# Pair-product ring of five PSUM banks instead of six, with the eighth bank given to attention and residuals

## The chip, the core and the metric

The kernel runs on one core of a Trainium2 chip. The metric is the device time of one execution in microseconds (us). Engines: PE (TensorE), with its weight load shown as PEld; DVE (VectorE); ACT (ScalarE); POOL (GpSimd); SP (SyncE), which issues DMAs. They run side by side and are ordered by semaphores. PSUM has eight banks of 128 partitions x 512 f32. PE writes its results there, DVE and ACT read them.

## What is computed

64 graphs of 128 nodes with 128 features. Cut to what matters:

```python
# layer 0, per graph: x, adj are 128 x 128
h   = relu(hi[:, None, :] + hj[None, :, :] + b1)     # 128 x 128 pairs x 128
y   = layernorm(h @ W2 + b2) * gamma + beta          # over the last axis
x1  = layernorm(x + einsum('ij,ijh->ih', adj, y))
# layer 1
e     = exp(si[:, None] + sj[None, :] + a_b) * adj
x_out = layernorm(x1 + (e / e.sum(1, keepdims=True)) @ x1)
```

## The kernel before, in words

All is f32 but a scratch tile of squares. The program is unrolled over 66 slots, t = 0 to 65 (`run_slots`, L156). In slot t three graphs are at work: the *pairs* of graph t (slots 0 to 63), the *gather* of graph t-1 (its layer norm statistics and the weighted sums over pairs) and the *tail* of graph t-2 (residual, layer norms, attention). *prep* prepares graph t+1. Slots 2 to 63 have pairs, gather and tail.

A slot has 16 units u of 8 rows i, and a unit has two quarts k of 4 rows. A quart goes through the engines like this:

- POOL (L278) adds hi and hj for a unit into `h`. ACT (L294) applies the relu in place, two units ahead of use.
- PE (L650, issued in the helper line L567) multiplies the quart by `w_pair` into one PSUM bank of the ring `y_ps`: 4 products, 32 matmul instructions in the trace, over four column tiles. Ahead of a unit it waits for `h_ready`, and ahead of quart k for `q_done >= t*QUARTS + k - YRING + 1` (L645), which says that DVE is through with the bank's earlier contents.
- ACT (L367, in the trace L289) copies the quart from the bank to `y` in SBUF.
- DVE (L553) multiplies bank and copy and sums the products into `q`: four instructions per quart, each followed by a read of the accumulator. The last one counts up `q_done`. DVE's code goes by (u, e), e = 0 to 3: e = 0, 1 are the halves of quart 2u, and e = 2, 3 those of quart 2u+1. A step at (u, e) stands ahead of that half's squares.

Between the quarts, at fixed places, stand the steps of gather and tail, in program order on each engine:

- DVE: variance `v` at (0,0), L449; the diagonal blocks of the sums into `o_sb` and `o_all` at (0,0) to (0,3), L460 to L468; `adj_sum` at (1,0), L455; `x1p` (gamma, mean and bias part) at (2,0), (2,1), (2,2), L476, L479, L483; x1p plus residual and its statistics at (4,0) to (4,2), L489 to L497; x1 and the two scores at (6,0) to (6,2), with the transposes for the next graph; `project`, the copy of the projections, at (9,0); attention's row sum, inverse and residual at (11,0) to (11,3); statistics at (12,0), (12,1); output at (14,0).
- ACT: `ln_v` and `rstd` at u = 1, `beta_part` at 2, the first root at 6, exponentials and `x1s` at 8, the second root at 14.
- POOL: weights `wz` at u = 5, `x_beta` at 6.
- PE: projections of the next graph at u = 9 (L631), attention at u = 11 (L638), and behind the pairs of units 4, 6, 7, 9, 10, 12, 13 and 15 one chunk of the weighted sums (L618), eight matmul instructions of 512 columns. The first chunk waits for `wz` and for L483 of the tail.

PSUM: six banks are the ring `y_ps` (the last of them also serves the setup), one is `agg_ps` (weighted sums), and one is `work_ps`. That one holds `v`, then attention `att` over the same columns, `z_e`, `z_r`, `x1p` (later `ab_ps`, the projections, over it) and `x2p`. Several engines use `work_ps`, so extra waits keep their steps apart: L475 (ln_v has read v before x1p is written), L630 and L635 on PE.

Of the kernel before, what the change touches and what calls it, by code (L numbers as in the profile page):

```python
# [33 lines left out]
def gnn_pair_kernel(nc, x, adj, W1, b1, W2, b2, gamma, beta, Ww, Wb, aw, ab, out):  # L34
# [4 lines left out]
    B, S, H = x.shape  # L39
    K = W2.shape[0]  # L40
# [6 lines left out]
    HRING = 4  # L47
    YRING = 6
    GROUPS, GROUP = 4, 32
# [13 lines left out]
    with ctx:  # L63
# [55 lines left out]
        agg_ps = ps("agg_ps", [S, 512])  # L119
        work_ps = ps("work_ps", [S, 512])  # L120
        setup_ps = y_ps[YRING - 1]
        v = work_ps[:, 0:K]
        att = work_ps[:, 0:K + 1]
        z_e, z_r = work_ps[:, K + 1:K + 2], work_ps[:, K + 2:K + 3]
        x1p, x2p = work_ps[:, 2 * K:3 * K], work_ps[:, 3 * K:4 * K]
        ab_ps = work_ps[:, 2 * K:4 * K].rearrange("k (m s) -> k m s", m=2)
# [160 lines left out]
        def _(act):  # L287
# [21 lines left out]
            def slot(t, half, p, pairs, prep, gather, tail, early, first_bank):  # L309
                for u in range(UNITS):  # L310
# [30 lines left out]
                    if tail and u == 8:  # L341
# [8 lines left out]
                        nc.scalar.activation(x1s[:], x1e[:], ACT.Identity, scale=e_ij[:, 1:2]).then_inc(x1s_ready, 1)  # L350
                    if tail and u == 14:

                        act.wait_ge(mv2_ready, t - 1)
                        nc.scalar.activation(ln2[:], mv2[:, 1:2], ACT.Ln, bias=epsc[:, 0:1]).then_inc(ln2_ready, 1)
                        act.wait_ge(ln2_ready, t - 1)
                        nc.scalar.activation(rs2[:], ln2[:], ACT.Exp, scale=-0.5).then_inc(rs2_ready, 1)  # L356
# [17 lines left out]
        def _(dve):  # L374
# [66 lines left out]
            def slot(t, half, p, pairs, prep, gather, tail, early, first_bank):  # L441

                for u, e in ((u, e) for u in range(UNITS) for e in range(2 * QPU)):
# [17 lines left out]
                    if tail and u == 0 and 1 <= e < CHUNK:  # L461
# [5 lines left out]
                        else:  # L467
                            nc.vector.scalar_tensor_tensor(out=o_all, in0=agg_ps[:, e * K:(e + 1) * K], scalar=part[:, e:e + 1],  # L468
                                                           in1=o_sb[:], op0=ALU.mult, op1=ALU.add,
                                                           accum_out=o_sum[:, 0:1]).then_inc(o_stored, 1)  # L470
                    if tail and (u, e) == (2, 0):
                        dve.wait_ge(o_stored, t - 1)
                        if gather:

                            dve.wait_ge(ln_v_ready, t)  # L475
                        nc.vector.tensor_tensor(x1p, o_all, gamma_rows[:], ALU.mult).then_inc(scaled_ready, 1)  # L476
                    if tail and (u, e) == (2, 1):
                        dve.wait_ge(scaled_ready, t - 1)
                        nc.vector.scalar_tensor_tensor(out=x1p, in0=mean_rows[:], scalar=o_sum[:, 0:1], in1=x1p,  # L479
                                                       op0=ALU.mult, op1=ALU.add).then_inc(mean_added, 1)  # L480
                    if tail and (u, e) == (2, 2):
                        dve.wait_ge(mean_added, t - 1)
                        nc.vector.scalar_tensor_tensor(out=x1p, in0=bias_rows[:], scalar=o_all[:, LAST:S], in1=x1p,  # L483
                                                       op0=ALU.mult, op1=ALU.add).then_inc(bias_added, 1)
# [27 lines left out]
                    if prep and (u, e) == (9, 0):  # L512
# [3 lines left out]
                        project(t + 1, 1 - p)  # L516
                    if tail and (u, e) == (11, 0):
                        dve.wait_ge(att_done, t - 1)
                        dve.wait_ge(e_ready, t - 1)
                        nc.vector.tensor_scalar(z_e, att[:, K:K + 1], e_ij[:, 0:1], None, ALU.mult).then_inc(z_e_ready, 1)  # L520
                    if tail and (u, e) == (11, 1):
                        dve.wait_ge(z_e_ready, t - 1)
                        nc.vector.reciprocal(z_r, z_e).then_inc(z_r_ready, 1)
                    if tail and (u, e) == (11, 2):
                        dve.wait_ge(z_r_ready, t - 1)
                        nc.vector.tensor_scalar(rz[:], z_r, e_ij[:, 0:1], None, ALU.mult).then_inc(rz_ready, 1)
                    if tail and (u, e) == (11, 3):
                        dve.wait_ge(rz_ready, t - 1)
                        dve.wait_ge(x1_ready, t - 1)
                        nc.vector.scalar_tensor_tensor(out=x2p, in0=att[:, 0:K], scalar=rz[:, 0:1], in1=x1e[:, 0:K],  # L530
                                                       op0=ALU.mult, op1=ALU.add).then_inc(x2p_ready, 1)
                    if tail and (u, e) == (12, 0):
                        dve.wait_ge(x2p_ready, t - 1)
                        nc.vector.bn_stats(st2[:], x2p).then_inc(st2_ready, 1)
                    if tail and (u, e) == (12, 1):
                        dve.wait_ge(st2_ready, t - 1)

                        dve.sem_inc(s_passed, 1)
                        nc.vector.bn_aggr(mv2[:], st2[:]).then_inc(mv2_ready, 1)
                    if tail and (u, e) == (14, 0):  # L540
                        dve.wait_ge(rs2_ready, t - 1)
# [21 lines left out]
        def _(pe):  # L563
# [58 lines left out]
            def slot(t, half, p, pairs, prep, gather, tail, early, first_bank):  # L622
                for u in range(UNITS):
                    if prep and u == 9:
                        if gather:

                            pe.wait_ge(ln_v_ready, t)
                        if tail:

                            pe.wait_ge(sj_ready, t - 1)  # L630
                        prep_products(t + 1, True)  # L631
                    if tail and u == 11:
                        if prep:

                            pe.wait_ge(ab_sb_s, t + 2)  # L635
                        pe.wait_ge(x1s_ready, t - 1)
# [49 lines left out]
```

## Time and profile before

| | |
|---|---|
| median of 3 runs | 2303.24 us (2301.99 to 2304.12) |
| the profiled execution | 2303.22 us |
| its span | 2301.4 us |
| PE, ACT, DVE, POOL busy | 99%, 94%, 93%, 88% |
| mean granted TensorE clock | 0.998 |

The span runs from the first to the last instruction of the trace; the rest of the time lies around it. Busy shares are averages over the span. The end of a matmul is modelled. Times in the rows are microseconds from the span's start.

### The profile page before, as it was taken

How to read it: one execution, taken by the hardware profiler on the slowest of the kernel's cores; microseconds unless marked ns; L12 is line 12 of the kernel's file. 1: busy time of each engine (PE TensorE's matmuls, PEld its weight loads, DVE VectorE, ACT ScalarE, POOL GpSimd, SP SyncE). 2: the span in 40 equal slices, each digit the busy share in tenths (PEclk: the TensorE clock that was granted, in tenths of full speed). 3: DMA queues.
4: the chain of work that ended last, by engine and by line, in shares of the span. 5: the costliest groups of instructions: out<-in, count | busy, mean ns of one | idle time of the engine just before them, and what ended most of it. 6: DMA issues, size and time to landing. Idle time of an engine off the chain costs nothing.

```text
span 2301.4 us, 168989 instructions
## 1 busy us (share of the span) xinstructions
PE 2280.2 (99%) x71248; PEld 2075.6 (90%) x71248; DVE 2145.2 (93%) x18262; ACT 2160.9 (94%) x3650; POOL 2016.9 (88%) x1227
## 2 busy tenths in 40 slices
PE   8999999999999999999999999999999999999997
PEld 8888888888888999999999999999999999999995
DVE  7999999999999999999999999999999999999998
ACT  8999999999999999999999999999999999999996
POOL 9898898888988988888888898898888988888884
PEclk9999999999999999999999999999999999999999
DMA  1000000000000000000000000000000000000000
GB/s 21 12 13 16 11 16 16 10 16 12 15 16 10 16 16 11 16 12 15 16 11 16 13 13 16 11 16 16 10 16 13 14 16 10 16 17 10 16 10 10
DMA packets 103862, 32.15 MB, mean 14 GB/s; under 512 B 77888, under 2 KB 103104, under 8 KB 103104
## 3 DMA queue, kind: packets, MB, share of 16 engines
q1 hardware_dynamic: 102240, 21.12, 4.4%
q8 instruction: 561, 9.19, 1.7%
q14 instruction: 197, 1.61, 0.2%
q10 hardware_dynamic: 864, 0.23, 0.0%
HBM read 17.11 MB, written 4.19 MB: 9 GB/s over the span
## 4 chain that ended last, share of the span: by engine, by line
PE 97%; ACT 2%; DVE 1%; POOL 0%; issue 0%; DMA 0%; SPq 0%; DVEq 0%; ACTq 0%
PE y_ps L567 76%; PE agg_ps L618 19%; PE work_ps L567 2%; ACT h L294 1%; ACT y L289 1%; POOL h L278 0%; DVE squares L553 0%; DMA b1c<-in_L_gnn_b_dram 0%; DVE o_sb L465 0%; DVE x_out L545 0%; POOL wz L269 0%; SPq L172 0%; DVE work_ps L483 0%; DVE work_ps L530 0%; DVE work_ps L479 0%
## 5 line engine op out<-in xcount | busy, mean ns | idle before, releaser
L278 POOL TENSOR_TENSOR h<-abT 128x1024 f32<-128x1024 f32 x1024 | 1944.0, 1919 | 239.3 <-PE y_ps L567 231.9
L567 PEld LDWEIGHTS y_ps<-w_pair,h 128*32 128x32 f32 x65536 | 1920.4, 110 | 173.6 <-issue 126.5
L567 PE MATMUL y_ps<-w_pair,h 128*32 128x128 f32 x65536 | 1966.0, 273 | 1.3 <-issue 0.6
L553 DVE CUSTOM_DVE_ANT_0 squares<-y_ps,y 128x128 bf16<-128x128 f32 x8192 | 1839.0, 284 | 110.4 <-ACT y L289 103.4
L289 ACT ACTIVATE y<-y_ps 128x508 f32<-128x508 f32 x2048 | 1137.5, 596 | 104.6 <-PE y_ps L567 97.6
L294 ACT ACTIVATE h<-h 128x1024 f32<-128x1024 f32 x1024 | 1089.3, 1064 | 2.4 <-POOL h L278 2.4
L553 DVE DVE_READ_ACCUMULATOR2_ANT q<- 128x1 f32 x8192 | 678.5, 83 | 0.0
L618 PE MATMUL agg_ps<-y,wz 128*32 128x512 f32 x4096 | 593.4, 592 | 3.2 <-DVE work_ps L483 3.1
L618 PEld LDWEIGHTS agg_ps<-y,wz 128*32 128x32 f32 x4096 | 180.4, 110 | 9.1 <-issue 9.1
L567 PEld LDWEIGHTS work_ps<-x1s,adjS 128*32 128x32 f32 x512 | 28.4, 110 | 31.5 <-issue 18.9
L252 POOL TENSOR_TENSOR wz<-adjT,rstd 128x128 f32<-128x128 f32 x64 | 34.8, 543 | 25.0 <-ACT rstd L325 25.0
L545 DVE TENSOR_SCALAR x_out<-work_ps,mv,rs 128x128 f32<-128x128 f32 x64 | 26.2, 410 | 27.5 <-ACT rs L356 27.5
L465 DVE SCALAR_TENSOR_TENSOR o_sb<-agg_ps,part,o_sb 128x128 f32<-128x128 f32 x128 | 44.3, 346 | 0.1
L567 PE MATMUL work_ps<-x1s,adjS 128*32 128x129 f32 x512 | 33.8, 275 | 6.4 <-ACT x1s L350 6.4
L264 POOL TENSOR_TENSOR x_beta<-beta_part,x_res 128x128 f32<-128x128 f32 x64 | 29.7, 464 | 10.4 <-ACT beta_part L334 10.4
L567 PE MATMUL work_ps<-xT,w1a 128*32 128x128 f32 x512 | 33.6, 275 | 4.4 <-DMA b1c<-in_L_gnn_b_dram 4.4
L567 PE MATMUL work_ps<-xT,w1b 128*32 128x128 f32 x512 | 33.6, 275 | 0.0
L334 ACT ACTIVATE beta_part<-beta_rows,adj_sum 128x128 f32<-128x128 f32 x64 | 25.7, 401 | 3.0 <-DVE adj_sum L455 3.0
L350 ACT ACTIVATE x1s<-x1e,e_ij 128x129 f32<-128x129 f32 x64 | 25.9, 405 | 2.1
L500 DVE TENSOR_SCALAR x1e<-work_ps,mv,rs 128x128 f32<-128x128 f32 x64 | 26.1, 407 | 1.2 <-ACT rs L340 1.2
L567 PEld LDWEIGHTS work_ps<-xT,w1a 128*32 128x32 f32 x512 | 22.5, 110 | 4.4 <-issue 4.4
L506 DVE CUSTOM_DVE_ANT_0 s_terms<-work_ps,v2row,score_c 128x128 f32<-128x128 f32 x64 | 26.1, 407 | 0.0
(87 smaller groups left out, 591.3 us busy)
## 6 DMA issues: line engine op xcount, KB each, us to landing
adj_in<-in_adj_dram SPq DMA_DIRECT2D x256, 16.0 KB, 1.9
x_res<-in_x_dram SPq DMA_DIRECT2D x64, 64.0 KB, 2.1
adj_res<-in_adj_dram SPq DMA_DIRECT2D x64, 64.0 KB, 2.7
out_dram<-x_out SPq DMA_DIRECT2D x64, 64.0 KB, 1.9
x_in<-in_x_dram SPq DMA_DIRECT2D x254, 16.0 KB, 1.9
w1a<-in_L_gnn_W_dram SPq DMA_DIRECT2D x1, 64.0 KB, 1.9
w1b<-in_L_gnn_W_dram ACTq DMA_DIRECT2D x1, 64.0 KB, 2.2
w<-in_L_gnn_W_dram ACTq DMA_DIRECT2D x1, 64.0 KB, 2.3
```

What stands on the lines that cost most here:

```text
L252: nc.gpsimd.tensor_tensor(columns, adjT[:, 1 - p, :].rearrange("j (g c s) -> j g c s", g=GROUPS, s=CHUNK), rstd[:].rearrange("j (c s g) -> ...
L264: nc.gpsimd.tensor_tensor(x_beta[:], beta_part[:], x_res[:, p, :], ALU.add).then_inc(x_beta_ready, 1)
L278: nc.gpsimd.tensor_tensor(h[:, u % HRING].rearrange("k (r g) s -> k r g s", g=GROUPS), abT[:, p, 1, :].unsqueeze(1).unsqueeze(1).broadcast ...
L289: return nc.scalar.activation(dst, src, ACT.Copy)
L294: nc.scalar.activation(h[:, u % HRING], h[:, u % HRING], ACT.Relu).then_inc(h_ready, 1)
L465: nc.vector.scalar_tensor_tensor(out=o_sb[:], in0=agg_ps[:, e * K:(e + 1) * K], scalar=part[:, e:e + 1], in1=o_sb[:], op0=ALU.mult, op1=AL ...
L500: nc.vector.tensor_scalar(x1e[:, 0:K], x1p, mv1[:, 0:1], rs1[:, 0:1], ALU.subtract, ALU.mult).then_inc(x1_ready, 1)
L506: nc.vector.tensor_tensor_reduce(out=s_terms[:, 0, :], in0=x1p, in1=v2row[:], scale=rs1[:, 0:1], scalar=score_c[:, 0:1], op0=ALU.mult, op1 ...
L545: nc.vector.tensor_scalar(x_out[:], x2p, mv2[:, 0:1], rs2[:, 0:1], ALU.subtract, ALU.mult).then_inc(out_ready, 1)
L553: last = nc.vector.tensor_tensor_reduce(out=squares[:, (first_bank + k) % YRING, n, :], in0=y_ps[(first_bank + k) % YRING][:, n, :], in1=y ...
L567: last = nc.tensor.matmul(dst[cols], lhsT[:, cols], rhs, start=start, stop=stop, tile_position=(0, g * GROUP))
L618: last = nc.tensor.matmul(agg_ps[g * GROUP:(g + 1) * GROUP, :], wz[:, g, chunk, :], y_chunk[:, :, g, :], start=(chunk == 0), stop=(chunk = ...
```

## The change

The ring has five banks, so PE waits for `q_done` of quart k-5. The freed bank is `att_ps` and takes `att`, `z_e`, `z_r`, `x1p` and `x2p`; `v` and `ab_ps` stay in `work_ps`. The three x1p steps on DVE stand at (1,1), (1,2), (1,3) in place of (2,0), (2,1), (2,2). Attention on PE is at u = 10 in place of 11, and the steps that follow from it stand one unit earlier: on DVE at 10, 11 and 13, on ACT the second root at 13. Three waits are gone: for `ln_v_ready` ahead of x1p, for `sj_ready` ahead of the projections, for `ab_sb_s` ahead of attention. `setup_ps`, the ring's last bank, is number 4 in place of 5.

```diff
--- before.py
+++ after.py
@@ -45,7 +45,7 @@
     QUARTS = S // QUART
     QPU = UNIT // QUART
     HRING = 4
-    YRING = 6
+    YRING = 5
     GROUPS, GROUP = 4, 32
     LAST = S - 1
 
@@ -117,12 +117,12 @@
 
         y_ps = [ps(f"y_ps{n}", [S, QUART, K]) for n in range(YRING)]
         agg_ps = ps("agg_ps", [S, 512])
-        work_ps = ps("work_ps", [S, 512])
+        work_ps, att_ps = ps("work_ps", [S, 512]), ps("att_ps", [S, 512])
         setup_ps = y_ps[YRING - 1]
         v = work_ps[:, 0:K]
-        att = work_ps[:, 0:K + 1]
-        z_e, z_r = work_ps[:, K + 1:K + 2], work_ps[:, K + 2:K + 3]
-        x1p, x2p = work_ps[:, 2 * K:3 * K], work_ps[:, 3 * K:4 * K]
+        att = att_ps[:, 0:K + 1]
+        z_e, z_r = att_ps[:, K + 1:K + 2], att_ps[:, K + 2:K + 3]
+        x1p, x2p = att_ps[:, 2 * K:3 * K], att_ps[:, 3 * K:4 * K]
         ab_ps = work_ps[:, 2 * K:4 * K].rearrange("k (m s) -> k m s", m=2)
         o_all = agg_ps[:, 0:K]
         b2c_ps, bnorm_ps = agg_ps[:, 3 * K:3 * K + 1], setup_ps[:, 3, 4:5]
@@ -348,7 +348,7 @@
                         act.wait_ge(e_ready, t - 1)
                         act.wait_ge(x1_ready, t - 1)
                         nc.scalar.activation(x1s[:], x1e[:], ACT.Identity, scale=e_ij[:, 1:2]).then_inc(x1s_ready, 1)
-                    if tail and u == 14:
+                    if tail and u == 13:
 
                         act.wait_ge(mv2_ready, t - 1)
                         nc.scalar.activation(ln2[:], mv2[:, 1:2], ACT.Ln, bias=epsc[:, 0:1]).then_inc(ln2_ready, 1)
@@ -468,17 +468,14 @@
                             nc.vector.scalar_tensor_tensor(out=o_all, in0=agg_ps[:, e * K:(e + 1) * K], scalar=part[:, e:e + 1],
                                                            in1=o_sb[:], op0=ALU.mult, op1=ALU.add,
                                                            accum_out=o_sum[:, 0:1]).then_inc(o_stored, 1)
-                    if tail and (u, e) == (2, 0):
+                    if tail and (u, e) == (1, 1):
                         dve.wait_ge(o_stored, t - 1)
-                        if gather:
-
-                            dve.wait_ge(ln_v_ready, t)
                         nc.vector.tensor_tensor(x1p, o_all, gamma_rows[:], ALU.mult).then_inc(scaled_ready, 1)
-                    if tail and (u, e) == (2, 1):
+                    if tail and (u, e) == (1, 2):
                         dve.wait_ge(scaled_ready, t - 1)
                         nc.vector.scalar_tensor_tensor(out=x1p, in0=mean_rows[:], scalar=o_sum[:, 0:1], in1=x1p,
                                                        op0=ALU.mult, op1=ALU.add).then_inc(mean_added, 1)
-                    if tail and (u, e) == (2, 2):
+                    if tail and (u, e) == (1, 3):
                         dve.wait_ge(mean_added, t - 1)
                         nc.vector.scalar_tensor_tensor(out=x1p, in0=bias_rows[:], scalar=o_all[:, LAST:S], in1=x1p,
                                                        op0=ALU.mult, op1=ALU.add).then_inc(bias_added, 1)
@@ -514,30 +511,30 @@
 
                             dve.wait_ge(u_ready, t * UNITS)
                         project(t + 1, 1 - p)
-                    if tail and (u, e) == (11, 0):
+                    if tail and (u, e) == (10, 0):
                         dve.wait_ge(att_done, t - 1)
                         dve.wait_ge(e_ready, t - 1)
                         nc.vector.tensor_scalar(z_e, att[:, K:K + 1], e_ij[:, 0:1], None, ALU.mult).then_inc(z_e_ready, 1)
-                    if tail and (u, e) == (11, 1):
+                    if tail and (u, e) == (10, 1):
                         dve.wait_ge(z_e_ready, t - 1)
                         nc.vector.reciprocal(z_r, z_e).then_inc(z_r_ready, 1)
-                    if tail and (u, e) == (11, 2):
+                    if tail and (u, e) == (10, 2):
                         dve.wait_ge(z_r_ready, t - 1)
                         nc.vector.tensor_scalar(rz[:], z_r, e_ij[:, 0:1], None, ALU.mult).then_inc(rz_ready, 1)
-                    if tail and (u, e) == (11, 3):
+                    if tail and (u, e) == (10, 3):
                         dve.wait_ge(rz_ready, t - 1)
                         dve.wait_ge(x1_ready, t - 1)
                         nc.vector.scalar_tensor_tensor(out=x2p, in0=att[:, 0:K], scalar=rz[:, 0:1], in1=x1e[:, 0:K],
                                                        op0=ALU.mult, op1=ALU.add).then_inc(x2p_ready, 1)
-                    if tail and (u, e) == (12, 0):
+                    if tail and (u, e) == (11, 0):
                         dve.wait_ge(x2p_ready, t - 1)
                         nc.vector.bn_stats(st2[:], x2p).then_inc(st2_ready, 1)
-                    if tail and (u, e) == (12, 1):
+                    if tail and (u, e) == (11, 1):
                         dve.wait_ge(st2_ready, t - 1)
 
                         dve.sem_inc(s_passed, 1)
                         nc.vector.bn_aggr(mv2[:], st2[:]).then_inc(mv2_ready, 1)
-                    if tail and (u, e) == (14, 0):
+                    if tail and (u, e) == (13, 0):
                         dve.wait_ge(rs2_ready, t - 1)
                         if early >= 3:
 
@@ -625,14 +622,8 @@
                         if gather:
 
                             pe.wait_ge(ln_v_ready, t)
-                        if tail:
-
-                            pe.wait_ge(sj_ready, t - 1)
                         prep_products(t + 1, True)
-                    if tail and u == 11:
-                        if prep:
-
-                            pe.wait_ge(ab_sb_s, t + 2)
+                    if tail and u == 10:
                         pe.wait_ge(x1s_ready, t - 1)
                         pe.wait_ge(adjS_ready, t - 1)
                         mm(att, adjS[:, p, :], x1s[:]).then_inc(att_done, 1)
```

## Rows read from the trace of the kernel before

**Rows 1.** The page: busy us (share of the span) and instructions of each engine

```profile
PE 2280.2 (99%) x71248; PEld 2075.6 (90%) x71248; DVE 2145.2 (93%) x18262; ACT 2160.9 (94%) x3650; POOL 2016.9 (88%) x1227
```

**Rows 2.** Chain that ended last, longest pieces: start us, us, what

```profile
77.39 8.73 PE y_ps L567 x320
112.86 8.73 PE y_ps L567 x320
...
2101.56 8.88 PE y_ps L567 x312
```

**Rows 3.** All waits in one slot, 1000 to 1036: who for whom, us, times, longest

```profile
POOL h L278 <- PE y_ps L567: 3.7, 6, 0.9
DVE squares L553 <- ACT y L289: 1.8, 4, 0.8
ACT y L289 <- PE y_ps L567: 1.5, 6, 0.4
DVE x_out L545 <- ACT rs L356: 0.4, 1, 0.4
POOL wz L252 <- ACT rstd L325: 0.3, 1, 0.3
```

**Rows 4.** Windows, L567 alone: busy us and instructions (x), granted clock

```profile
1000.17:1007.18 7.01, 7.01 (x256) 7.01 (x256) 1.00 0.19 40
```

**Rows 5.** Windows, two whole slots: busy us of each engine, granted clock

```profile
1000.17:1035.64 35.47, 35.47 (x1117) 33.03 (x1112) 33.48 (x286) 33.71 (x58) 31.50 (x20) 1.00 0.06 13
1035.64:1071.91 36.27, 35.86 (x1117) 32.98 (x1113) 33.46 (x286) 34.02 (x58) 31.48 (x20) 1.00 0.06 14
```

**Rows 6.** Timeline, weight load ahead of the first sums of the slot: start us, us

```profile
1008.79 0.15 PEld L618 LDWEIGHTS agg_ps<-y,wz 128*32 128x32 f32 x3
```

**Rows 7.** Timeline, the matmuls of the same instructions

```profile
1008.90 0.63 PE L618 MATMUL agg_ps<-y,wz 128*32 128x512 f32 x3
```

**Rows 8.** Timeline, DVE in units 1, 2 and 4: start us, us, line, operation

```profile
1005.85 0.08 DVE L553 DVE_READ_ACCUMULATOR2_ANT q<- 128x1 f32 x1
...
1006.69 0.08 DVE L553 DVE_READ_ACCUMULATOR2_ANT q<- 128x1 f32 x1
1006.69 0.29 DVE L476 TENSOR_TENSOR work_ps<-agg_ps,gamma_rows 128x128 f32<-128x128 f32 x1
1007.16 0.29 DVE L553 CUSTOM_DVE_ANT_0 squares<-y_ps,y 128x128 bf16<-128x128 f32 x1 [0.17 <-ACT y L289]
...
1007.59 0.35 DVE L479 SCALAR_TENSOR_TENSOR work_ps<-mean_rows,o_sum,work_ps 128x128 f32<-128x128 f32 x1
1007.85 0.28 DVE L553 CUSTOM_DVE_ANT_0 squares<-y_ps,y 128x128 bf16<-128x128 f32 x1
...
1008.27 0.08 DVE L553 DVE_READ_ACCUMULATOR2_ANT q<- 128x1 f32 x1
...
1012.30 0.09 DVE L553 DVE_READ_ACCUMULATOR2_ANT q<- 128x1 f32 x1
```

**Rows 9.** Timeline, set-up: DVE releases a weight load

```profile
6.23 0.28 DVE L417 COPY w2T<-y_ps 128x128 f32<-128x128 f32 x1
...
6.57 0.20 PEld L567 LDWEIGHTS agg_ps<-basis,w2T 128*32 128x32 f32 x8 [0.99 <-DVE w2T L417]
```

**Rows 10.** Timeline, drain: DVE releases the sums

```profile
2281.73 0.36 DVE L483 SCALAR_TENSOR_TENSOR work_ps<-bias_rows,agg_ps,work_ps 128x128 f32<-128x128 f32 x1
...
2282.21 0.19 PEld L618 LDWEIGHTS agg_ps<-y,wz 128*32 128x32 f32 x8 [3.96 <-issue]
2282.24 1.06 PE L618 MATMUL agg_ps<-y,wz 128*32 128x512 f32 x8 [3.08 <-DVE work_ps L483]
```

**Rows 11.** Timeline, PE at the second chunk of sums

```profile
1013.25 0.63 PE L618 MATMUL agg_ps<-y,wz 128*32 128x512 f32 x3
```

**Rows 12.** Timeline, weight loads in slot 1

```profile
48.92 1.69 PEld L567 LDWEIGHTS y_ps<-w_pair,h 128*32 128x32 f32 x64 [0.74 <-ACT h L294]
```

**Rows 13.** Timeline, DVE in slot 1, the end of quart 4

```profile
50.24 0.08 DVE L553 DVE_READ_ACCUMULATOR2_ANT q<- 128x1 f32 x1
```

## The prediction, made before the changed kernel was run

> **What bounds the kernel now.** Start with the busy table [rows 1]: PE is busy 99% of the span, ACT 94%, DVE 93%, POOL 88%. Busy PE time is modelled, so it proves nothing alone. The chain of work that ended last [rows 2] goes by PE nearly throughout, and its pieces repeat: 320 matmuls of the pair product in one unbroken piece of 8.73 us, and the next such piece starts 35.47 us later (112.86 - 77.39). Then read the waits of one slot [rows 3]: POOL, ACT and DVE wait for PE (3.7 and 1.5 us) or for each other, and no line has PE or its weight load waiting. The windows [rows 5] say the same: 35.47 us of a slot, 35.47 us of PE. So in a steady slot PE streams without a stall, at a granted clock of 1.00, and any stall that the change puts into PE's stream is paid in full, once per slot. For the same reason nothing can be won by taking away a wait of PE that is already met.
>
> I call a bank's worth of rows a quart (four rows i, 32 matmul instructions). A slot has 32 quarts, two to a unit. From [rows 4], 256 matmuls, which is quarts 0 to 7, fill 7.01 us from the slot's start at 1000.17. So quart 8 starts at 1007.18 and quart 9 at 1008.05, 0.87 us each. PE loads weights 0.11 us ahead of the matmul (1008.79 against 1008.90, [rows 6, 7]), and the wait sits on the first weight load. So the loads that the waits hold stand at about 1007.07 (quart 8) and 1007.94 (quart 9).
>
> **The ring, six to five.** L645 lets PE write quart k when DVE has squared quart k-6. With five banks it is k-5, which is one quart, 0.87 us, less lead. Where is DVE furthest behind? In units 0 to 2 of a slot it has the tail's work between its squares. DVE's timeline [rows 8] gives the ends. L476 stands ahead of quart 4's first square, so quart 3 ended at 1006.69 + 0.08 = 1006.77. Four squares earlier, at a pitch of 0.21, quart 2 ended at 1005.85 + 0.08 = 1005.93. Quart 4 starts at 1007.16, takes four pitches and L479, and ends at 1008.27 + 0.08 = 1008.35. With six banks quart 9 needs quart 3 (1006.77 against 1007.94: 1.17 us in hand). With five it needs quart 4: 1008.35 is 0.41 us after the load wants to go. Quart 8 needs quart 3: 0.30 us in hand. So with the ring alone one wait per slot appears, at quart 9.
>
> How long from DVE's end to PE's load? The trace of before has no wait of PE on squares. The nearest rows [rows 9, 10]: w2T ends at 6.51 and the load starts at 6.57 (0.06); L483 ends at 2282.09 and the load of the sums starts at 2282.21 (0.12). I take 0.09. There the matmul follows the released load by 0.03 us, not 0.11, so about 0.1 us of a late load is absorbed by the lead. The ring alone: 0.41 + 0.09 - 0.10 = 0.40 us per slot.
>
> **The x1p chain moved from unit 2 to unit 1.** L476, L479 and L483 now stand ahead of half-quarts (1,1), (1,2) and (1,3), so one lies inside quart 2 and two ahead of the halves of quart 3. What one inserted step costs DVE is the distance to the next square [rows 8]: 0.26 us for L479 (1007.59 to 1007.85), and the same for L483, which has its form. L476 lasts 0.29 us, as a square does, so I give it the square's pitch, 0.21. Quart 2 ends 0.21 later (1006.14; quart 7's load wants 1006.20, so with 0.06 to 0.12 of release up to 0.06 late, and I fold that into what follows). Quart 3 ends 0.73 later: 1007.50. Nothing absorbs this: four squares in 0.84 us are back to back. The 0.17 us that DVE idles ahead of quart 4 [rows 8] lies behind it.
>
> So quart 8's load, which needs quart 3, goes at 1007.50 + 0.09 = 1007.59 in place of 1007.07, and its matmul at about 1007.61 in place of 1007.18: 0.43 us late. Quart 4: its first square goes at 1006.69 + 0.73 = 1007.42 (the copy is done by 1007.16), its last read ends after four pitches of 0.21 and 0.08 at 1008.34, the same as before, since the three steps are now ahead of it. Quart 9's load may go at 1008.43. PE, already late, wants it at 1007.61 + 0.87 - 0.11 = 1008.37, so 0.06 more, most of it within the lead; I add 0.03. **0.46 us per slot.** Quart 5 ends 0.2 us earlier than before, and the next tight place is quart 13, which needs quart 8: done at 1012.30 + 0.09 = 1012.39 [rows 8], and its load stands at 1013.25 - 0.87 - 0.11 = 1012.27 [rows 11]. That is 0.12 short today and is covered once PE is 0.46 late. So the stalls don't add up, the first one pays for the others. ACT lags there: DVE gets the copy of quart 4 at 1007.16, and PE had started the last matmul of that quart by 1000.17 + 5 x 0.87 = 1004.5. So ACT doesn't feel PE's delay. POOL waits for PE in six places of a slot [rows 3]; I take it that none of them leads back to PE within the slot. By the end of a slot everyone waits for PE again and the slot starts as before.
>
> **The split of the banks.** PE loses its wait for sj_ready ahead of the projections and for ab_sb_s ahead of attention; L476 loses the wait for ln_v_ready. In a steady slot no engine stands on any of them [rows 3]: worth 0. Attention one unit earlier: the same eight matmuls. z_e to bn_aggr in units 10 and 11, ln2 and rs2 in 13: the same instructions, at places where DVE and ACT themselves wait for PE [rows 3]. They are the cover, and 0.2 to 0.3 us per step would show only if it were gone. No DMA is moved. In the drain (slots 64 and 65) attention goes ahead of a chunk of sums and DVE's chain ends earlier, but DVE then waits for PE's last sums: 0.1 us gained at most.
>
> **The first slots.** The setup bank is now bank 4, so PE waits for s_ready one quart earlier, but L435 had long ended. In slots 0 and 1 ACT sets the pace: quart 8 of slot 1 starts at 48.92 released by ACT's h [rows 12]. Quart 9's load wants about 49.7, and quart 4 ends at 50.24 + 0.08 = 50.32 [rows 13]. So PE leaves this stretch about 0.6 us later, once (0 to 1).
>
> The trace shows 0.11 us from load to matmul [rows 6, 7]. The Trainium skill ("TensorE: Matmul & The Clock Gate", Part 2, step by step) says that PE takes weight loads ahead of running matmuls out of a queue of 64. If a load held by a wait could be passed that far, the whole 0.46 us would hide, and the time would be (c) below; the 0.11 us speaks for only a quarter of it.
>
> **The sum.** Steady slots with both pairs and a tail are t = 2 to 63, 62 of them. 62 x 0.46 = 28.5; start +0.6; drain -0.1; in all +29.0. The profiled execution took 2303.22 us, 2301.4 of them span, within 0.02 of the median 2303.24, so it stands for the median. 2303.2 + 29.0 = 2332.2, 1.3% slower.
>
> **The rivals.**
> (a) The forecast, one stall per slot at quart 8 or 9. Bounds per slot: from 0.34 (release 0.06, ring alone, lead of 0.13) to 0.62 (release 0.12, nothing absorbed): 21 to 38 us, and up to 1 at the start. 2324 to 2343. The ring alone, 0.40, would give 2328.6, so both parts of the change lead into this range. Chance 0.78.
> (b) The stalls add up: PE, late at quart 8, delays POOL and ACT's relu of later units so that quart 13 and later ones are late as well. For it: ACT has little room (94%). Against it: ACT is over 2 us behind PE at quart 4 [rows 8]. A second stall of the same size gives 62 x 0.9 = 56: about 2360. Chance 0.08.
> (c) The stall is hidden, same time: DVE's lag at quart 3 is regained, or the load's lead swallows it. That would need less than 0.07 us per slot in place of 0.46. Time 2303 to 2307. Against it: 0.41 us short at quart 9 is read off two rows. Chance 0.11.
> (d) Faster: PE's waits at units 9 and 11 for DVE (sj_ready) and for abT (ab_sb_s) cost something in the slots that are longer than 35.47 us, such as that from 1035.64 to 1071.91 (36.27 us, 35.86 of PE) [rows 5]. It would have to give over 5 us, and the ring to cost nothing. But from the piece at 77.39 to that at 2101.56 there are 57 slots in 2024.17 us [rows 2], and 57 x 35.47 = 2021.8: all the longer ones together hold 2.4 us. With all of it back: 2301. Chance 0.03.
> The rule to have all 8 PSUM banks in use (the Trainium skill, "Perfetto Trace Analysis", Matmul Optimizations) sees no difference, since both kernels use eight; by it the result would be (c). The trace speaks of the six and five that rotate.
>
> **How the numbers follow.** The likeliest is (a) at 2332. Its own range is 2324 to 2343; to hold 8 in 10 I widen it a little for slots whose stall is smaller or larger than in the one that I read: 2320 to 2346. A measurement of this kernel can tell about 0.2% (4.6 us). Slower is (a) and (b) and a sliver of (c): 0.87; same is most of (c) and of (d): 0.11; faster 0.02.
>
> **What would show it.** In the trace after: the slot's pitch at 35.9 to 36.0 us; in the list of waits PE or its weight load waiting for DVE squares L553, about 62 times, 0.3 to 0.5 us each; the unbroken piece of 320 matmuls cut at 256; quart 3 of a slot ending 0.7 us later. Wrong: a pitch of 35.47 with these waits absent (c); the stall at two places (b); or a wait of PE on something else.

## The result, and the profile after

| | before | after |
|---|---|---|
| median | 2303.68 us (4 runs) | 2325.53 us (4 runs) |
| ratio, 95% interval | | 1.0097 (1.0085 to 1.011) |
| profiled execution, its span | 2303.22, 2301.4 us | 2324.8, 2322.9 us |
| busy PE / DVE / ACT / POOL | 99 / 93 / 94 / 88% | 99 / 93 / 93 / 87% |

The changed kernel is 21.9 us slower, 1.0%. I had forecast 2332 (2320 to 2346). The busy table, to be held against [rows 1], and the chain's shares by engine, after:

```profile
PE 2292.5 (99%) x71248; PEld 2003.7 (86%) x71248; DVE 2162.6 (93%) x18262; ACT 2166.8 (93%) x3650; POOL 2016.7 (87%) x1227
...
PE 73%; DVE 20%; ACT 6%; issue 1%; POOL 0%; DMA 0%; SPq 0%; DVEq 0%; ACTq 0%
```

PE is still "99% busy", as before. The chain tells the two apart: before, PE held 97% of it, and now PE holds 73% and DVE 20%. Here is one slot of the chain of work that ended last in the changed kernel (start, length, what; "..." marks pieces left out), to be held against [rows 2]:

```profile
1045.38 0.29 DVE squares L550
...
1050.89 0.21 DVE att_ps L473
...
1051.51 0.27 DVE att_ps L476
...
1052.18 0.27 DVE att_ps L480
...
1053.02 1.95 PE y_ps L564 x64
1054.97 0.86 PE agg_ps L615 x8
...
1079.16 0.59 ACT y L289
...
1080.70 0.49 ACT y L289
```

The slot begins with DVE. From 1045.38 to about 1052.9 the chain is its squares with the tail's steps between them, up to L480 (the lines L473, L476 and L480 of this kernel are L476, L479 and L483 of the kernel before). At 1053.02, at quart 8, it goes over to PE and stays there for 26 us, until ACT's copies at 1079.16 and 1080.70 lead to DVE's squares of the next slot. In [rows 2] PE's piece ran unbroken through quarts 0 to 9.

The same place on PE (matmuls) and on the weight load, in the timeline of the changed kernel:

```profile
1045.66 7.20 PE L564 MATMUL y_ps<-w_pair,h 128*32 128x128 f32 x256
1053.02 1.95 PE L564 MATMUL y_ps<-w_pair,h 128*32 128x128 f32 x64 [0.16 <-DVE q L550]
```

```profile
1045.66 6.93 PEld L564 LDWEIGHTS y_ps<-w_pair,h 128*32 128x32 f32 x252 [0.27 <-issue]
1052.99 1.72 PEld L564 LDWEIGHTS y_ps<-w_pair,h 128*32 128x32 f32 x64 [0.40 <-issue]
```

```profile
1081.50 7.20 PE L564 MATMUL y_ps<-w_pair,h 128*32 128x128 f32 x256
1088.85 1.41 PE L564 MATMUL y_ps<-w_pair,h 128*32 128x128 f32 x44 [0.15 <-DVE q L550]
```

The piece of 320 matmuls is cut at 256, as the forecast had said. Quart 8 starts 1053.02 - 1045.66 = 7.36 us into the slot (7.35 in the next slot), where it started after 7.01 us before [rows 4]. The slot's pitch is 1081.50 - 1045.66 = 35.84 us, before 35.47: 0.37 us more. In slots 2 to 20 of the kernel before, and in ring5_alone, quart 8 starts at 6.99 (medians), and 7.36 - 6.99 is 0.37, so all of the slot's loss lies at this one place. And DVE's end of quart 3, in its timeline:

```profile
1050.80 0.30 DVE L473 TENSOR_TENSOR att_ps<-agg_ps,gamma_rows 128x128 f32<-128x128 f32 x1
1051.00 0.28 DVE L550 CUSTOM_DVE_ANT_0 squares<-y_ps,y 128x128 bf16<-128x128 f32 x1
...
1051.42 0.35 DVE L476 SCALAR_TENSOR_TENSOR att_ps<-mean_rows,o_sum,att_ps 128x128 f32<-128x128 f32 x1
1051.68 0.29 DVE L550 CUSTOM_DVE_ANT_0 squares<-y_ps,y 128x128 bf16<-128x128 f32 x1
...
1052.10 0.36 DVE L480 SCALAR_TENSOR_TENSOR att_ps<-bias_rows,agg_ps,att_ps 128x128 f32<-128x128 f32 x1
1052.36 0.29 DVE L550 CUSTOM_DVE_ANT_0 squares<-y_ps,y 128x128 bf16<-128x128 f32 x1
...
1052.79 0.09 DVE L550 DVE_READ_ACCUMULATOR2_ANT q<- 128x1 f32 x1
```

Quart 3's last read ends at 1052.79 + 0.09 = 1052.88, PE's held load starts at 1052.99. [rows 8] shows the first two of the three steps before, in unit 2.

A reader who looks for the stall in the list of waits of the whole kernel finds little of it under its own name:

```profile
PEld y_ps L564 <- issue: 235.2, 845, 0.7
...
PE y_ps L564 <- DVE q L550: 9.0, 56, 0.4
```

62 slots times 0.37 us is 23 us, and the list has 9.0 us (56 times) for the matmul waiting for DVE. The weight load's idle of 0.40 us at 1052.99 goes to "issue", whose sum grew from 126.5 us, on the page before, to 235.2. The matmuls' own row hides part of the gap, too: their ends are modelled, and the piece of 256 is shown 7.20 us long where the pace of [rows 4] gives 7.01. The chain and the place where a regular pattern is cut were the views that found it.

The start: slot 2 began at 77.21 us with slot 0 at 9.84 before, and now

```profile
9.88 18.18 PE L564 MATMUL y_ps<-w_pair,h 128*32 128x128 f32 x574
...
77.85 7.17 PE L564 MATMUL y_ps<-w_pair,h 128*32 128x128 f32 x256
```

that is 67.97 us in place of 67.37, or 0.6 us more, once. It doesn't come about at one place. Quart 4 of slot 0 starts 4.46 us into the slot, before 5.54, because PE went over from 1.69 to 0.87 us a quart earlier in this execution, for a reason that no row shows. From quart 9 on the ring holds PE already in slot 0, as here:

```profile
19.21 1.75 PEld L564 LDWEIGHTS y_ps<-w_pair,h 128*32 128x32 f32 x64 [0.40 <-DVE q L550]
```

Slot 1 starts 0.87 us later than before, and within slot 1 0.28 us of that is regained.

### The profile page after: what moved, and what is told of

Its sections match the earlier page's. It is cut to its first block, busy times and chain, and to the rows that moved or that the text cites. A ratio compares the mean times of both kernels' runs of the same rounds, so it can differ in the third digit from the quotient of the medians.

```text
span 2322.9 us, 168866 instructions
## 1 busy us (share of the span) xinstructions
PE 2292.5 (99%) x71248; PEld 2003.7 (86%) x71248; DVE 2162.6 (93%) x18262; ACT 2166.8 (93%) x3650; POOL 2016.7 (87%) x1227
## 4 chain that ended last, share of the span: by engine, by line
PE 73%; DVE 20%; ACT 6%; issue 1%; POOL 0%; DMA 0%; SPq 0%; DVEq 0%; ACTq 0%
PE y_ps L564 54%; PE agg_ps L615 17%; DVE squares L550 12%; ACT y L289 3%; ACT h L294 3%; DVE o_sb L465 1%; PE work_ps L564 1%; DVE q L550 1%; DVE work_ps L449 1%; DVE agg_ps L468 1%; DVE att_ps L480 1%; DVE att_ps L476 1%; DVE o_sb L460 1%; PE att_ps L564 1%; DVE att_ps L473 1%
## 5 line engine op out<-in xcount | busy, mean ns | idle before, releaser
L564 PEld LDWEIGHTS y_ps<-w_pair,h 128*32 128x32 f32 x65536 | 1845.5, 110 | 259.4 <-issue 235.2
L564 PE MATMUL y_ps<-w_pair,h 128*32 128x128 f32 x65536 | 1930.7, 273 | 10.5 <-DVE q L550 9.0
L615 PE MATMUL agg_ps<-y,wz 128*32 128x512 f32 x4096 | 550.7, 592 | 3.2 <-DVE att_ps L480 3.2
L615 PEld LDWEIGHTS agg_ps<-y,wz 128*32 128x32 f32 x4096 | 142.3, 110 | 8.2 <-issue 8.2
L564 PEld LDWEIGHTS att_ps<-x1s,adjS 128*32 128x32 f32 x512 | 21.2, 110 | 39.9 <-issue 31.6
L564 PE MATMUL att_ps<-x1s,adjS 128*32 128x129 f32 x512 | 28.7, 275 | 6.2 <-ACT x1s L350 6.2
L542 DVE TENSOR_SCALAR x_out<-att_ps,mv,rs 128x128 f32<-128x128 f32 x64 | 26.3, 412 | 5.6 <-ACT rs L356 1.2
L497 DVE TENSOR_SCALAR x1e<-att_ps,mv,rs 128x128 f32<-128x128 f32 x64 | 26.2, 410 | 3.3 <-ACT rs L340 1.2
L503 DVE CUSTOM_DVE_ANT_0 s_terms<-att_ps,v2row,score_c 128x128 f32<-128x128 f32 x64 | 26.1, 407 | 0.0
L320 ACT ACTIVATE ln_v<-work_ps,epsc 128x128 f32<-128x128 f32 x64 | 23.4, 366 | 2.4 <-DVE work_ps L449 2.4
```

The source lines that it names most:

```text
L497: nc.vector.tensor_scalar(x1e[:, 0:K], x1p, mv1[:, 0:1], rs1[:, 0:1], ALU.subtract, ALU.mult).then_inc(x1_ready, 1)
L503: nc.vector.tensor_tensor_reduce(out=s_terms[:, 0, :], in0=x1p, in1=v2row[:], scale=rs1[:, 0:1], scalar=score_c[:, 0:1], op0=ALU.mult, op1 ...
L542: nc.vector.tensor_scalar(x_out[:], x2p, mv2[:, 0:1], rs2[:, 0:1], ALU.subtract, ALU.mult).then_inc(out_ready, 1)
L564: last = nc.tensor.matmul(dst[cols], lhsT[:, cols], rhs, start=start, stop=stop, tile_position=(0, g * GROUP))
L615: last = nc.tensor.matmul(agg_ps[g * GROUP:(g + 1) * GROUP, :], wz[:, g, chunk, :], y_chunk[:, :, g, :], start=(chunk == 0), stop=(chunk = ...
```

## The experiments

Each is compared with the kernel before on the same chip. "Pitch" is the distance from one slot's first pair matmul to the next one's, which stays the same over most slots of a run.

| kernel | ring | pitch, us | median, us | ratio to before |
|---|---|---|---|---|
| before | 6 | 35.47 | 2303.7 | |
| after | 5 | 35.84 | 2325.5 | 1.0097 (1.0085 to 1.011) |
| ring5_alone | 5 | 35.73 | 2320.5 | 1.0073 (1.0057 to 1.009) |
| x1p_early_ring6 | 6 | 35.47 | 2303.9 | 0.9998 (0.9988 to 1.0007) |
| x1p_back_ring5 | 5 | 35.73 | 2320.5 | 1.007 (1.0055 to 1.0085) |
| relieved | 5 | 35.47 | 2304.8 | 1.0006 (0.9996 to 1.0015) |
| ring4 | 4 | 36.68 | 2379.4 | 1.0335 (1.0318 to 1.0352) |
| one_more_step | 5 | 36.03 | 2339.1 | 1.016 (1.0144 to 1.0175) |
| one_more_step_ring6 | 6 | 35.47 | 2303.8 | 1.0003 (0.9994 to 1.0013) |
| attention_early_ring6 | 6 | 35.79 | 2321.6 | 1.0084 (1.0069 to 1.0099) |
| x1p_spread | 5 | 35.64 | 2319.2 | 1.0066 (1.0051 to 1.0081) |
| beta_late | 5 | 35.47 | 2306.0 | 1.001 (1.000 to 1.0019) |
| x1p_placed | 5 | 35.48 | 2307.7 | 1.0014 (1.0005 to 1.0023) |

Theory R says that the cost is PE's wait for DVE's squares of quart k-5, and nothing else. Rival C says that it is the x1p chain's earlier place.

### The ring alone

```diff
--- before
-    YRING = 6
+    YRING = 5
```

> The kernel before with five ring banks and nothing else; the eighth bank lies unused, all waits and places are the old ones. Theory R (the ring's wait on DVE's squares is the whole cost): one stall per slot at quart 9, which now needs quart 4. Quart 4 ends 0.41 us after quart 9's weight load wants to go, release 0.12 as in the changed kernel, some 0.1 absorbed by the lead: pitch 35.47 + 0.43, in all about +25 us, 2328. Rival C (the x1p chain, put earlier on DVE, is what costs): it is at its old place here, so the time stays within 5 us of before.

Measured: 2320.5, +16.9 us. The ring by itself costs, so rival C falls as the whole cause. The size is below the 25 us that I expected. The weight loads at quart 9, and DVE:

```profile
1016.10 0.81 PEld L567 LDWEIGHTS y_ps<-w_pair,h 128*32 128x32 f32 x32 [0.32 <-DVE q L553]
```

```profile
1014.39 0.08 DVE L553 DVE_READ_ACCUMULATOR2_ANT q<- 128x1 f32 x1
...
1015.96 0.08 DVE L553 DVE_READ_ACCUMULATOR2_ANT q<- 128x1 f32 x1
```

```profile
1008.00 9.18 PE L567 MATMUL y_ps<-w_pair,h 128*32 128x128 f32 x320
```

```profile
1043.73 9.18 PE L567 MATMUL y_ps<-w_pair,h 128*32 128x128 f32 x320
```

Quart 4 ends at 1015.96 + 0.08 = 1016.04, and the load follows at 1016.10, 0.06 us later. The slot starts at 1008.00, so quart 4 ends 8.04 us into it, where I had read 1008.35 - 1000.17 = 8.18 in the slot of [rows 8]. Pitch 1043.73 - 1008.00 = 35.73: 0.26 us per slot in place of 0.40.

### The x1p steps early, with six banks

```diff
--- before
-                    if tail and (u, e) == (2, 0):
+                    if tail and (u, e) == (1, 1):
...
-                    if tail and (u, e) == (2, 1):
+                    if tail and (u, e) == (1, 2):
...
-                    if tail and (u, e) == (2, 2):
+                    if tail and (u, e) == (1, 3):
```

> The kernel before, six ring banks, with only the three x1p steps moved to unit 1 (their wait for ln_v_ready stays). Theory R: quart 9 needs quart 3, which ends 0.7 us later but still 0.4 us before the load wants to go: pitch 35.47, time within 3 us of before. Rival C: the moved chain costs by itself, pitch about 35.8, +20 us.

Measured: 2303.9, no difference. With six banks the early chain is free. Its wait for ln_v_ready stood in this kernel, so that wait, which the split removes, is met as well.

### The x1p steps late, with five banks

```diff
--- after
-                    if tail and (u, e) == (1, 1):
+                    if tail and (u, e) == (2, 0):
...
-                    if tail and (u, e) == (1, 2):
+                    if tail and (u, e) == (2, 1):
...
-                    if tail and (u, e) == (1, 3):
+                    if tail and (u, e) == (2, 2):
```

> The changed kernel with the x1p steps back in unit 2. Theory R: the stall moves from quart 8 to quart 9 and keeps its size within 0.05 us, since quart 4 ends at the same time either way: pitch 35.80 to 35.88, 2324 to 2328. Rival C: the stall at quart 8 came of the moved chain, so it goes: near 2304.

Measured: 2320.5. The stall moved to quart 9, but it didn't keep its size: the pitch is 35.73, below the 35.80 to 35.88 that I expected, and equal to that of the ring alone. So of the 0.37 us, the ring costs 0.26 with the x1p steps where they were, and their earlier place adds 0.10, about 5 us in all. It adds them only because the ring has five banks. ring5_alone and x1p_back_ring5 differ in the bank split, the waits and attention's place, and have the same pitch and time: these parts are worth nothing here.

### One more step on DVE, with five banks and with six

```diff
--- after, and x1p_early_ring6
                         dve.wait_ge(o_stored, t - 1)
+                        nc.vector.tensor_tensor(spare[:], o_all, gamma_rows[:], ALU.mult)
                         nc.vector.tensor_tensor(x1p, o_all, gamma_rows[:], ALU.mult).then_inc(scaled_ready, 1)
```

`spare` is a new tile in SBUF that nobody reads. With six banks the wait for ln_v_ready stands between the first two lines.

> The changed kernel with one more DVE step of L476's kind at (1,1), written to a spare tile in SBUF that nobody reads. Theory R: quart 3 ends 0.21 us later and PE stands at it, so the pitch grows by that much, 35.83 to 36.04, and the time by 62 x 0.21 = 13 us to about 2338. Rival (each stall has a price of its own, such as restarting PE's stream, whatever its length): the time stays within 2 us of the changed kernel, 2325.

> Six ring banks, one bank for attention and variance, x1p steps in unit 1 with their old wait, and the same additional DVE step at (1,1). Theory R: quart 9 needs quart 3, which now ends at 7.51 us of the slot, with release 7.63, and the load wants to go at 7.79: nothing, pitch 35.47, 2304. Rival (DVE's load counts, whatever the ring): +13 us as with five banks.

Measured: 2339.1 and 2303.8. Slots in the timelines of PE:

```profile
1051.92 7.20 PE L566 MATMUL y_ps<-w_pair,h 128*32 128x128 f32 x256
...
1087.95 7.20 PE L566 MATMUL y_ps<-w_pair,h 128*32 128x128 f32 x256
```

```profile
999.59 9.00 PE L569 MATMUL y_ps<-w_pair,h 128*32 128x128 f32 x317
...
1035.06 9.00 PE L569 MATMUL y_ps<-w_pair,h 128*32 128x128 f32 x317
```

Pitch 36.03 with five banks and 35.47 with six. The additional 0.2 us of DVE comes out one to one in the slot with five banks (36.03 - 35.84 = 0.19) and not at all with six. That rules out a fixed price for each stall and also DVE's load as such.

### Four banks

```diff
--- after
-    YRING = 5
+    YRING = 4
```

> The changed kernel with four ring banks. Theory R, from the trace of the changed kernel: quart 7 then needs quart 3, which ends 7.27 us into the slot, 0.12 of release makes 7.39, and quart 7's load wants to go at 6.03: 1.36 late, 0.1 absorbed. Quart 8 then needs quart 4 (8.12 + 0.12) and PE, already late, wants it at 8.24: no more. So again one stall pays for all: pitch 35.47 + 1.25 = 36.7, 2380 to 2390 in all. Rival (stalls add up, as DVE and ACT fall behind with PE): well over 2400. Rival (cost in proportion to banks taken away): pitch 35.47 + 2 x 0.36 = 36.2, about 2349.

Measured: 2379.4, just under the range that I gave, pitch 36.68, or 1.21 us over that of six banks: close to the 1.25 that came from two ends in the trace of the changed kernel, and far from both rivals. The weight loads in one slot (start, length):

```profile
1037.56 0.81 PEld L564 LDWEIGHTS y_ps<-w_pair,h 128*32 128x32 f32 x32 [0.35 <-DVE q L550]
1038.86 0.84 PEld L564 LDWEIGHTS y_ps<-w_pair,h 128*32 128x32 f32 x32 [0.48 <-issue]
1040.16 2.62 PEld L564 LDWEIGHTS y_ps<-w_pair,h 128*32 128x32 f32 x96 [0.46 <-DVE q L550]
```

and the matmuls:

```profile
1032.91 5.74 PE L564 MATMUL y_ps<-w_pair,h 128*32 128x128 f32 x192
...
1040.17 2.89 PE L564 MATMUL y_ps<-w_pair,h 128*32 128x128 f32 x96 [0.19 <-DVE q L550]
```

Quarts 5, 6 and 7 each start late. Without a stall quart 7 starts 6.11 us into the slot and quart 8 at 6.99 (medians in ring5_alone). Here quart 7 starts at 1040.17 - 1032.91 = 7.26, 1.15 late, and quart 8 at 8.20 (median of all slots), 1.21 late: the 0.06 that quart 8 adds, where I had expected none, doesn't show as a gap of its own. What counts is the largest of "DVE's end of quart k-4, less the time at which PE would want quart k"; here quarts 7 and 8 are nearly level and quart 8 is the last. The stalls of one slot don't add up beyond it.

### Relief ahead of quart 4

On POOL `x_beta`, on ACT `beta_part`, and on DVE the x1p steps:

```diff
--- after
-    POOL_WEIGHTS_UNIT, POOL_RESIDUAL_UNIT = 5, 6
+    POOL_WEIGHTS_UNIT, POOL_RESIDUAL_UNIT = 5, 7
...
-                    if tail and u == 2:
+                    if tail and u == 3:
...
-                    if tail and (u, e) == (1, 1):
+                    if tail and (u, e) == (2, 0):
...
-                    if tail and (u, e) == (1, 2):
+                    if tail and (u, e) == (2, 2):
...
-                    if tail and (u, e) == (1, 3):
+                    if tail and (u, e) == (2, 3):
```

> The changed kernel with DVE and ACT relieved ahead of quart 4: x1p steps at (2,0), (2,2), (2,3), beta_part on ACT at unit 3 in place of 2, x_beta on POOL at unit 7 in place of 6. Theory R: quart 3 then ends 0.27 us before quart 8's load wants to go and quart 4, no longer held by ACT's beta_part, ends about 0.2 us before quart 9's: the stall goes, pitch 35.47 to 35.55, 2303 to 2309, with five banks. If the time stays near 2325, the number of banks costs in another way than by these two quarts.

Measured: 2304.8, 1.0006 (0.9996 to 1.0015), pitch 35.47. Five banks cost nothing per slot once the first five quarts are ready in time. The next two kernels take this one apart.

`x1p_spread` has only the x1p steps of the diff above.

> The changed kernel with the x1p steps at (2,0), (2,2), (2,3) and nothing else moved, beta_part back at unit 2. Theory R: quart 4 is held by ACT's copy until 6.85 us into the slot, but L479 no longer lies inside it: it ends at 7.78 in place of 8.04, release makes 7.84, and quart 9's load wants to go at 7.75. 0.09 late is within what PE absorbs: pitch 35.47 to 35.52, 2303 to 2307. If it is near 2312, ACT's copy was half of the stall and beta_part had to move too.

Measured: 2319.2. This missed, and in a third place. The chain of waits of this kernel, in a slot:

```profile
1114.44 8.73 PE y_ps L564 x320
1123.18 1.03 PE agg_ps L615 x8
...
1127.70 0.86 PE agg_ps L615 x8
```

The 320 matmuls of quarts 0 to 9 are whole again, so the ring's stall is gone. But the first chunk of sums takes 1.03 us where every other takes 0.86: 0.17 us per slot. PE waits there for L480, the last x1p step, which my expectation had left out. The timelines of DVE and of the weight load:

```profile
1014.98 0.36 DVE L480 SCALAR_TENSOR_TENSOR att_ps<-bias_rows,agg_ps,att_ps 128x128 f32<-128x128 f32 x1
```

```profile
1015.45 0.11 PEld L615 LDWEIGHTS agg_ps<-y,wz 128*32 128x32 f32 x1
```

L480 ends at 1015.34, 8.76 us into the slot that starts at 1006.58, and the load of the sums starts at 1015.45. In the kernel relieved, where the x1p steps stand at the same places, L480 ends 0.2 us earlier in the slot (median), since ACT's copy of quart 4 comes 0.2 us earlier there.

`beta_late` has only the POOL and ACT lines of the diff, with the x1p steps at (2,0), (2,1), (2,2).

> The changed kernel with the x1p steps back at (2,0), (2,1), (2,2), and beta_part on ACT at unit 3, x_beta on POOL at unit 7. Theory R: ACT's copy of quart 4 is 0.3 us earlier, quart 4 starts at 6.62 in place of 6.85 and ends, with L479 inside, at 7.80 in place of 8.04; release 7.86 against 7.75: 0.11 late, about what PE absorbs: pitch 35.47 to 35.55, 2303 to 2309. If ACT is not what holds quart 4, the stall stays: pitch 35.73, 2320.

Measured: 2306.0, pitch 35.47. With `beta_part` behind quarts 4 and 5, ACT's copy of quart 4 starts 5.95 us into the slot in place of 6.23 (medians; x1p_back_ring5 has the same x1p places), and the stall that x1p_back_ring5 had is gone. So ACT, not DVE alone, held quart 4. `x_beta` was moved with `beta_part`, which it reads; no run moves one alone.

### The x1p steps at the places that both waits allow

```diff
--- after
-                    if tail and (u, e) == (1, 1):
+                    if tail and (u, e) == (1, 3):
...
-                    if tail and (u, e) == (1, 2):
+                    if tail and (u, e) == (2, 0):
...
-                    if tail and (u, e) == (1, 3):
+                    if tail and (u, e) == (2, 2):
```

> The changed kernel with the x1p steps at (1,3), (2,0), (2,2); all else as changed. It asks whether the 0.17 us per slot that the spread placement kept is PE's first chunk of sums waiting for the last x1p step, L480, which then ended 8.76 us into the slot, while the chunk's load wants to go at 8.62. Here L480 stands one half-quart earlier and ends near 8.1. Quart 3 ends at 6.68, quart 8's load wants 6.88; quart 4 ends near 7.80, release 7.86, quart 9's load wants 7.75 and absorbs that. If the chunk's wait was the rest: pitch 35.47 to 35.50, 2303 to 2307, with five banks and the x1p steps alone moved. If not, the pitch stays at 35.64, near 2319.

Measured: 2307.7, pitch 35.48. Both waits are gone but for 0.01 us per slot. Moving three steps by two or three half-quarts gives back 18 of the 22 us. The ratio, 1.0014 (1.0005 to 1.0023), leaves some 3 us, of which the pitch explains 0.6. In the profiled execution the rest lies mostly in the drain: from slot 63 to the end it took 60.7 us, the profiled kernel before 57.7. Here are the sums of slot 64, first in x1p_placed, then in the kernel before:

```profile
2283.96 6.59 PE L615 MATMUL agg_ps<-y,wz 128*32 128x512 f32 x32 [3.19 <-DVE att_ps L480]
...
2290.59 3.62 PE L615 MATMUL agg_ps<-y,wz 128*32 128x512 f32 x32
```

```profile
2282.24 4.50 PE L618 MATMUL agg_ps<-y,wz 128*32 128x512 f32 x40 [3.08 <-DVE work_ps L483]
```

and the window from 2284 to 2288 in the same order (length, then busy us and instructions of PE, PEld, DVE, ACT and POOL, then the granted clock):

```profile
2284.00:2288.00 4.00, 4.00 (x20) 1.05 (x24) 1.71 (x8) 1.11 (x4) 0.00 (x0) 0.50 0.02 4
```

```profile
2284.00:2288.00 4.00, 4.00 (x48) 1.59 (x44) 1.64 (x9) 0.61 (x2) 0.00 (x0) 1.00 0.00 0
```

PE had waited 3.19 us for L480, and 3.08 us in the kernel before. In x1p_placed the granted clock then stood at 0.50, the lower of its two levels (1.2 GHz), and 32 sums took 6.59 us where the next 32 took 3.62. In the kernel before it was 1.00 in this window. The profiled x1p_spread (6.56 us for those 32 sums), relieved, beta_late and x1p_back_ring5 (5.34 each) show it too, and that is part of what their times have above their pitches. So does x1p_early_ring6 (6.20 us for 40 sums, against 4.50), which has six banks, so this remainder isn't the ring's. Why the clock fell after one such wait and not after the other stays open, and so does how often it does in the executions without a profile.

### Attention one unit earlier in one shared bank

```diff
--- before
-                    if tail and u == 11:
+                    if tail and u == 10:
                         if prep:
                             pe.wait_ge(ab_sb_s, t + 2)
```

The steps at 11, 12 and 14 on DVE and at 14 on ACT are one unit earlier in the same way.

> The kernel before, six ring banks and one bank for variance, projections and attention, with attention and what follows from it one unit earlier (places 10, 11 and 13) and its wait for ab_sb_s kept. It asks what the split of the banks buys. PE wants attention's first load 20.9 us into the slot, where quart 20's load stands; DVE ends the copy of the projections at 21.8: PE's load 0.9 us late, some 0.4 of it absorbed by the load's lead behind the 512-column sums. Pitch 35.47 + 0.5 to 0.6, 2330 to 2345. If the wait is met earlier than I read, 2304.

Measured: 2321.6, pitch 35.79, 0.32 per slot in place of 0.5 to 0.6, so the time is below the range that I gave. The mechanism is as expected:

```profile
1030.03 0.16 PEld L567 LDWEIGHTS work_ps<-x1s,adjS 128*32 128x32 f32 x8 [1.02 <-DVE abT L396]
```

```profile
1029.63 0.34 DVE L396 TENSOR_SCALAR abT<-work_ps,b1c 128x128 f32<-128x128 f32 x1
```

DVE ends the copy of the projections at 1029.97, 0.2 us earlier in the slot than I had reckoned, and PE's load of attention follows at 1030.03. So the split of the banks does buy something: it makes attention at unit 10 free, which in one shared bank costs 19 us (0.84%). But nothing in the kernel gains from attention being at unit 10, and at unit 11 the old wait was free, too.

## Why the prediction was right, and where its size was off

- **PE bounds the kernel and a stall is paid in full per slot.** Right. 62 x 0.37 + 0.6 = 23.5, against a span that grew by 21.5. The slots of the two traces settle the rest: from slot 2 to slot 63 the pitches above the usual one add up to 2.9 us before and to 1.0 us after, so 1.9 us of irregular slots are missing in the changed kernel. Why they are shorter there, chance or the stall's cover, no run isolates.
- **The wait moves by one quart, and the x1p chain moves it from quart 9 to quart 8.** Right. The piece of 320 is cut at 256 in the changed kernel and at quart 9 in ring5_alone.
- **Inserted steps cost 0.21, 0.26 and 0.26 us.** Measured 0.20, 0.26 and 0.26: 1050.80 to 1051.00, 1051.42 to 1051.68, 1052.10 to 1052.36.
- **Quart 3 ends 7.33 us into the slot** (1007.50 - 1000.17). This term was mis-sized: it ended at 1052.88 - 1045.66 = 7.22. The steps cost what I said, so DVE itself stood 0.1 us earlier in the slot. I had read its lag in a late slot of a stream without a stall. In ring5_alone the same end of quart 3, without inserted steps, is 1014.47 - 1008.00 = 6.47, against 6.60 in [rows 8]. x1p_early_ring6, with the three steps inserted and six banks, has both numbers in one trace: quart 3 ends at 7.21 in slots 2 to 20 and at 7.35 in the later ones (medians). The last section goes on from here.
- **Release 0.09, bounds 0.06 and 0.12.** Measured 0.06 (ring5_alone) and 0.11 (the changed kernel).
- **A late load loses 0.1 us less than its lateness.** Right: the load was at 7.33 us of the slot in place of 6.90, and the matmul 0.35 late, not 0.43. The 0.03 that I had added at quart 9 did not appear: the pitch grew by no more than quart 8's delay.
- **Per slot 0.46, measured 0.37.** 0.11 too much from the end of quart 3 and 0.03 for quart 9. Too little were 0.02 from the release, 0.01 from load to matmul (0.03, not 0.02), and 0.02 because quart 8 stands at 6.99 and not at 7.01 in a slot of this stream: 0.46 - 0.14 + 0.05 = 0.37. For the ring alone 0.40 was reckoned and 0.26 measured, by the same error of 0.14 in the end of quart 4 (8.04, not 8.18).
- **The stalls don't add up.** Right, and ring4 shows it with a stall three times as long.
- **The lost waits are worth nothing.** Right: x1p_back_ring5, with the split, and ring5_alone, without it, have the same time.
- **Once 0.6 us at the start.** Measured 0.6, and that is luck. The forecast had ACT set the pace in slots 0 and 1 and one new wait at quart 9 of slot 1. In the trace the ring already holds PE from quart 9 of slot 0 on (the load at 19.21, above, released by DVE's squares after 0.40 us), slot 1 starts 0.87 us late, and part of that is regained. Other traces differ here by as much as the whole term: ring5_alone lost 1.2 us.
- **The sign in the list of waits: about 62 times, 0.3 to 0.5 us each.** Only in part: 56 times, 0.16 us on average, for the reason given with the list. The pitch and the cut at 256 were the signs that held.
- **Rivals.** (b), the stalls add up, (c), it is hidden, and (d), faster, are all out by the pitch. The Trainium skill ("TensorE: Matmul & The Clock Gate", Part 2, step by step) says that PE pulls weight loads ahead of running matmuls. In this trace that did not carry a load past the wait that held it: the load itself started 0.43 us late.

## What to carry to other kernels

In a kernel whose bound engine streams without a gap, the depth of a ring is to be judged by a subtraction at each position: when does the producer want buffer k, and when does the consumer end k-N? Here only the largest shortfall of a period was paid, and it was paid every period. One bank less cost between 0 and 1% here, by the placing of three small steps of DVE and one of ACT, which had nothing to do with the ring but stood ahead of the wrong quart. When steps are moved to get rid of one wait, list all who wait for them: x1p_spread freed the ring and ran into the sums' wait for L480.

## What the runs showed that I had not expected

In a slot of the kernel before ACT's first copy, which waits for PE, starts 1.32 us after the slot's first matmul, and in ring5_alone 1.18 us:

```profile
1001.49 0.59 ACT L289 ACTIVATE y<-y_ps 128x508 f32<-128x508 f32 x1
```

```profile
1009.18 0.59 ACT L289 ACTIVATE y<-y_ps 128x508 f32<-128x508 f32 x1
```

(1001.49 - 1000.17 and 1009.18 - 1008.00.) DVE and all that follows is earlier by the same 0.14 us in the slot. In the kernel before itself it was still 1.18 in slot 2:

```profile
78.39 0.60 ACT L289 ACTIVATE y<-y_ps 128x508 f32<-128x508 f32 x1
```

(78.39 - 77.21.) The traces of all slots show when it changes. In the kernel before it is 1.18 to 1.20 in slots 2 to 20 and 1.29 or more from slot 21 on. At the same slot the order of the records changes. In slot 2 the eight matmuls of a chunk of sums stand together; later three of them are recorded ahead of the last pair matmul of the piece before, as here behind the three of [rows 7]:

```profile
85.94 1.04 PE L618 MATMUL agg_ps<-y,wz 128*32 128x512 f32 x8
```

```profile
1008.98 0.27 PE L567 MATMUL y_ps<-w_pair,h 128*32 128x128 f32 x1
```

The changed kernel gets such slots, too (7, 44 and 50 are at 1.30 to 1.35), and one or two slots later it is back at 1.20. beta_late and x1p_placed, whose pitch is that of six banks within 0.01 us but whose load of quart 9 is held in every slot, have 1.18 or 1.19 as their median. So the recorded start of a slot comes to lie some 0.12 to 0.14 us further ahead of its result after some of the irregular slots, and a held load in the next slots takes that back. A shortfall that is read off a late slot of a stream without a held load is too large by this much. Such a slot is worth comparing with one of the first. Whether PE really starts earlier there, or only its record does, stays open.
